# Ids prepared as pairs of 16 bit numbers, six banks for the first group's counts, two count blocks moved by one instruction

## The reference

```
mask   = (sequence_ids != 0)                                  # 2048 users x 200 ids
pooled = sum over the ids of item_embeddings[max(id - 1, 0)] * mask / max(number of ids that are not 0, 1)
user_rep  = pooled @ W_rec.T + b_rec
retrieved = item_embeddings[retrieved_indices].mean(axis=1)   # 50 per user
gate   = sigmoid(concat(user_rep, retrieved) @ gate_W.T + gate_b)
fused  = gate * user_rep + (1 - gate) * retrieved
logits = fused @ proj_W.T + proj_b                            # 2048 x 12500
```

## Time and profile before

| | us |
|---|---|
| median of 3 timed runs | 2159.99 (2159.94 to 2164.19) |
| the profiled execution | 2149.49 |
| its span (first to last instruction) | 2147.7 |
| TensorE busy | 2066.8 (96%) |
| VectorE busy | 1569.8 (73%) |
| ScalarE busy | 817.0 (38%) |
| GpSimd busy | 1126.0 (52%) |

### The profile page before, as it was taken

How to read it: one execution, slowest core, us unless ns; L and a number is a source line. 1 busy time by engine, 2 the same in 40 slices (tenths; PEclk the granted TensorE clock), 3 DMA queues, 4 the chain that set the end, 5 groups by cost and what they waited for, 6 DMA issues and landing times.

```text
span 2147.7 us, 32019 instructions
## 1 busy us (share of the span) xinstructions
PE 2066.8 (96%) x12722; PEld 1062.3 (49%) x12722; DVE 1569.8 (73%) x1677; ACT 817.0 (38%) x1009; POOL 1126.0 (52%) x830
## 2 busy tenths in 40 slices
PE   5669999999999999999999999999999999999999
PEld 4555555555555555444444444444444444444444
DVE  8999999888888887444577777687778864544544
ACT  5866676445544545435211212232212122221121
POOL 5676551788678855657366767666676500000000
PEclk8569999999999999999999999999999999999999
DMA  8999997999899988879589998887899974576665
GB/s 304 333 235 299 280 321 251 301 264 252 242 266 250 250 303 281 309 243 338 170 299 324 312 315 300 301 279 260 316 327 350 367 246 149 196 232 235 222 224 182
DMA packets 222050, 586.82 MB, mean 273 GB/s; under 512 B 21840, under 2 KB 121040, under 8 KB 218576
## 3 DMA queue, kind: packets, MB, share of 16 engines
q1 hardware_dynamic: 91424, 264.21, 36.2%
q0 software_dynamic: 77632, 218.16, 35.8%
q10 hardware_dynamic: 52848, 102.41, 12.6%
HBM read 448.21 MB, written 136.48 MB: 272 GB/s over the span
## 4 chain that ended last, share of the span: by engine, by line
PE 80%; DVE 8%; POOL 6%; ACT 3%; issue 2%; DVEq 2%; DMA 1%; ACTq 0%
PE banks_ps L1345 45%; PE banks_ps L1238 23%; PE banks_ps L1220 6%; PE banks_ps L1250 6%; POOL gathered L586 4%; DVE row_hots L685 2%; POOL gathered L564 2%; ACT counts L1003 2%; DVE keys L687 2%; DVE ring L692 1%; ACT counts L997 1%; DVEq L729 0%; DMA gathered<-emb,ret_rows 0%; PE banks_ps L1268 0%; DVE gathered L730 0%
## 5 line engine op out<-in xcount | busy, mean ns | idle before, releaser
L1238 PE MATMUL banks_ps<-mid,ring 128*128 128x512 f16 x3136 | 725.0, 379 | 1.7 <-ACT mid L1021 1.7
L564 POOL DMA_INDIRECT gathered<-emb,ret_rows x460 | 569.5, 1238 | 292.8 <-DVE gathered L730 137.2
L1345 PE MATMUL banks_ps<-counts,keys 128*128 128x500 f16 x2400 | 510.5, 374 | 0.0
L1345 PE MATMUL banks_ps<-counts,mid 128*128 128x500 f16 x2400 | 508.4, 374 | 1.5 <-DVE counts L776 1.5
L1238 PEld LDWEIGHTS banks_ps<-mid,ring 128*128 128x128 f16 x3136 | 292.0, 98 | 306.9 <-issue 3.2
L586 POOL DMA_INDIRECT gathered<-emb,ret_rows x184 | 348.1, 1892 | 130.0 <-ACT ring L1011 55.3
L963 DVE SCALAR_TENSOR_TENSOR ring<-banks_ps,out_scale,counts 128x1000 f32<-128x1000 f32 x160 | 201.1, 1257 | 259.7 <-PE banks_ps L1345 258.4
L1345 PEld LDWEIGHTS banks_ps<-counts,mid 128*128 128x128 f16 x2400 | 233.0, 97 | 274.0 <-DVE counts L776 2.0
L685 DVE TENSOR_TENSOR row_hots<-pair_columns,keys 128x2048 f16<-128x2048 f16 x256 | 313.0, 1223 | 71.2 <-PE banks_ps L1220 70.1
L1345 PEld LDWEIGHTS banks_ps<-counts,keys 128*128 128x128 f16 x2400 | 231.6, 97 | 269.6 <-DVE counts L776 0.2
L1220 PE MATMUL banks_ps<-keys,row_hots 128*128 128x98 f16 x4096 | 282.4, 225 | 59.4 <-DVE keys L687 44.5
(11 more groups left out here) (130 smaller groups left out, 878.0 us busy)
## 6 DMA issues: line engine op xcount, KB each, us to landing
logits<-ring ACTq DMA_DIRECT2D x99, 1000.0 KB, 6.5
ring<-emb_parts SPq DMA_DIRECT2D x147, 512.0 KB, 6.3
counts<-proj_t SPq DMA_DIRECT2D x75, 1000.0 KB, 5.7
counts<-emb SPq DMA_DIRECT2D x14, 1792.0 KB, 10.5
emb_parts<-ring SPq DMA_DIRECT2D x49, 512.0 KB, 6.4
mid<-emb SPq DMA_DIRECT2D x46, 512.0 KB, 7.4
counts<-proj_b SPq DMA_DIRECT2D x75, 250.0 KB, 4.6
gathered<-emb,ret_rows POOLq DMA_INDIRECT x660, 6.3
```

The source lines that it names most:

```text
L564: pool.indirect_dma_start(slots[group][:, a], None, source, column(block, r * SLOT + a))\
L1238: last = pe.matmul(pooled_ps[:, m], ring_v[:, p % RING, c, part, m * P:(m + 1) * P], cvt[:, p % CVT, c], start=(i == 0 and c == 0 and part ...
L1345: last = pe.matmul(banks_ps[:, logit_bank(n), 0:W], fused[g // 2][:, f, k, at_user:at_user + P], strip_parts[:, t % 2, w, k, :], start=(k ...
```

## The change

**Ids.** `prepare_ids` had eight instructions on 1024 elements of 32 bit inputs: subtract 1, find ids of 0 (as 512, added to the row so that it meets no column), find present ids, clamp, low bits, high bits, add, convert. It now has one with two tensors (negative ids wrap once, as `max((x < 0), x)` writes it), one that clamps, subtracts 1 and writes 16 bit numbers, two bitwise ones that work on pairs of these as 32 bit words (512 elements), and three on 16 bit numbers in and out (rows, chunks, present). An absent id is -1 now, whose chunk of 127 meets none of the 98 columns. The wait for `present_counted` stands ahead of the last of them, behind the two conversions.

**Banks.** The quads of group 0 use six banks, 1 to 6, in turn, and a quad waits for the move of the quad six before it. Later groups use banks 4 to 6 as before; their first three quads wait for all quads of group 0.

**Move.** In group 0 ScalarE moves a unit's two quads, from two neighbouring banks, by one instruction of 784 elements (`move_first`). The pieces of the table are squared after the same units as before: where one stood between a unit's two quads it now stands behind the unit.

```diff
+FIRST_BANKS = 6
+BOTH = (P - 1) * 65537
+        item_i = part_of(keys, 0, 2048, I16)
+        row_i = part_of(keys, 2048, 2048, I16)
+        asked_i = part_of(keys, 4096, 4096, I32)
+        column_i = part_of(keys, 4096, 2048, I16)
...
+        def first_bank(q):
+            return 1 + q % FIRST_BANKS
+        def count_bank(q):
+            return first_bank(q) if q < pl.quads else KH + q % COUNT_BANKS
...
             def prepare_ids(g):
                 dve.drain()
                 dve.wait_ge(ids_in, 16 * (g + 1))
-                dve.tensor_scalar(chunk_of, raw, -1.0, None, ALU.add)
-                dve.tensor_scalar(chunk_key, raw, 0.0, ABSENT, ALU.is_equal, ALU.mult)
+                dve.scalar_tensor_tensor(asked_i, raw, 0.0, raw, ALU.is_lt, ALU.max)
+                dve.drain()
+                dve.tensor_scalar(item_i, asked_i, float(pl.items), -1.0, ALU.min, ALU.add)
+                dve.drain()
+                dve.tensor_scalar(row_i.bitcast(I32), item_i.bitcast(I32), BOTH, None, ALU.bitwise_and)
+                dve.tensor_scalar(column_i.bitcast(I32), item_i.bitcast(I32), 7, BOTH, ALU.logical_shift_right,
+                                  ALU.bitwise_and)
+                dve.drain()
+                dve.tensor_copy(row_key, row_i)
+                dve.tensor_copy(chunk_key, column_i)
                 if g > 0:
                     dve.wait_ge(present_counted, g)
-                dve.tensor_scalar(present[:], raw, 0.0, None, ALU.not_equal)
-                dve.drain()
-                dve.tensor_scalar(clamped, chunk_of, 0.0, float(pl.items - 1), ALU.max, ALU.min)
-                dve.drain()
-                dve.tensor_scalar(raw, clamped, P - 1, None, ALU.bitwise_and)
-                dve.tensor_scalar(clamped, clamped, 7, None, ALU.logical_shift_right)
-                dve.drain()
-                dve.tensor_tensor(row_key, raw, chunk_key, ALU.add)
-                dve.drain()
-                dve.tensor_copy(chunk_key, clamped)
+                dve.tensor_scalar(present[:], item_i, -1.0, None, ALU.not_equal)
                 dve.drain().then_inc(ids_ready, 1)
...
+            def move_first(u):
+                act.wait_ge(quad_counted, 2 * (u + 1))
+                at = first_bank(2 * u)
+                act.activation(counts_v[:, 0, :, u * UNIT:(u + 1) * UNIT].rearrange("p c (b u) -> p c b u", b=2),
+                               banks_ps[:, at:at + 2, 0:QUAD * NQ].rearrange("p b (u c) -> p c b u", u=QUAD),
+                               ACT.Copy).then_inc(quad_moved, 2)
...
-            for q in range(pl.quads):
-                move_quad(q)
-                if q % 7 == 6 and squared < NORM:
+            for u in range(pl.units):
+                move_first(u)
+                if squared < min(NORM, 2 * (u + 1) // 7):
                     square_norm(squared)
                     squared += 1
-                if q in (119, 121, 123):
-                    if q == 119:
+                if u in (59, 60, 61):
+                    if u == 59:
                         act.wait_ge(scale_made, 1)
-                    split_high((q - 119) // 2)
+                    split_high(u - 59)
...
             def count_quad(q):
                 pe.wait_ge(hots_made, q // 2 + 1)
-                if q >= COUNT_BANKS:
-                    pe.wait_ge(quad_moved, q - COUNT_BANKS + 1)
+                if q >= pl.quads:
+                    pe.wait_ge(quad_moved, max(pl.quads, q - COUNT_BANKS + 1))
+                elif q >= FIRST_BANKS:
+                    pe.wait_ge(quad_moved, q - FIRST_BANKS + 1)
...
-                    to = count_ps[:, q % COUNT_BANKS, u * NQ:(u + 1) * NQ]
+                    to = banks_ps[:, count_bank(q), u * NQ:(u + 1) * NQ]
```

More of the change, by code:

```diff
@@ L11 @@
 I32 = mybir.dt.int32
+I16 = mybir.dt.int16
 U8 = mybir.dt.uint8
@@ L36 @@
 COUNT_BANKS = 3
-ABSENT = 512.0
+FIRST_BANKS = 6
+BOTH = (P - 1) * 65537
 F16_TOP = 14
@@ L221, in pooling_program @@
         raw = part_of(keys, 0, 4096, I32)
-        chunk_of = part_of(keys, 4096, 4096, F32)
-        clamped = part_of(keys, 4096, 4096, I32)
+        item_i = part_of(keys, 0, 2048, I16)
+        row_i = part_of(keys, 2048, 2048, I16)
+        asked_i = part_of(keys, 4096, 4096, I32)
+        column_i = part_of(keys, 4096, 2048, I16)
         row_key = part_of(keys, 8192, 2048, F16)
```

## The result

The changed kernel takes 2167.11 us (median of 22, one disturbed execution of 3621.36 among them; the others took 2163.86 to 2174.48, and the ratio is of these), the kernel before beside it 2161.19. The ratio is 1.0022, 95% interval 1.0012 to 1.0033. Forecast were 2150.4 us and 2144 to 2157: wrong in size and in sign.

What follows compares the result with a forecast made beforehand. VectorE was taken to bound the kernel up to some 220 us, TensorE behind that. The terms 6.65 + 1.26 - 0.33 + 0.72 + 1.26 = 9.56 us gave 2150.4 us, range 2144 to 2157.

Steps and rivals of the forecast that it cites:

- VectorE sets the pace up to 220 us: From the start to some 220 us VectorE is the limit, TensorE behind that; VectorE's losses ahead of pass 0 move the end.
- the stalls: First stage: six banks remove all waits around the table's squares, 0.95 us in each of 7 periods, 6.65 us gained.
- First ids: First preparation of ids, ahead of the first one-hots: 6.22 us becomes 4.96, 1.26 saved; bounds 2.8 saved to 0.4 lost.
- rival D: Preparation of ids: 16 bit instructions run at twice the rate, 0.44 us each, total 2149.6 us; chance 24%.
- The last move: ScalarE's last move ahead of pass 0 takes 0.83 us instead of 0.50: 0.33 us lost, bounds 0 and 0.5.
- rival A: First stage: the two-bank move is dear and ScalarE becomes the bound; 2165 us at twice the time per element; chance 6%.
- Group 1's stalls: Pass 0's start: shorter preparation of group 1 removes TensorE's stalls of 0.41 and 0.31 us, 0.72 us gained.
- Rival C: Start of pass 0: TensorE's half clock lasts into it by 16 products, 3.5 us lost, total 2153.9 us; chance 12%.
- Group 3's gathers: Pass 2: group 3's add comes earlier, so GpSimd's gathers land earlier: 1.26 us gained, bounds 0 and 1.32.
- rival E: Pass 2: the gathers behind group 3's preparation take no part, their term is 0, total 2151.7 us; chance 12%.
- What is late next is VectorE itself: First stage: once its stalls go, VectorE's own work sets the pace; ScalarE and TensorE keep up; no size of its own.
- Rival B: First stage: loads of the table's pieces set the pace, so the 6.65 us stay away, total 2157.0 us; chance 10%.

Runs made afterwards that it cites:

- e1_ids: The kernel before with the new preparation of ids alone (three banks, single moves): ratio 0.9976 to the kernel before, median 2156.74 us.
- e10_drain40: The changed kernel with one single drain of VectorE, ahead of unit 40: 2148.77 us, ratio 0.9950 to the kernel before.
- e9_sbuf: The kernel before with group 0's one-hots reading their columns as 32 bit numbers from SBUF: 2298.83 us, read for its trace alone.
- e6_drain8: The changed kernel with a drain of VectorE ahead of every eighth unit of group 0 (seven drains): ratio 0.9967 to the kernel before.
- e5_banks: The kernel before with six banks for group 0, old preparation of ids and single moves: 0.40% slower than the kernel before.
- e7_gate10: The changed kernel with each turn of GpSimd's gathers released by the tenth unit instead of the ninth: a gather held for 73.89 us; no total time given.
- e0_noids: The changed kernel with the old preparation of ids (six banks, two-bank moves): 0.55% slower than the kernel before.

## Why the prediction was wrong

- **VectorE sets the pace up to 220 us, and the stalls are worth 6.65 us: right.** Start of the stage 8.99 to 146.15 is 137.16 us, before 142.91, 5.75 less. The dearer move took 0.38 of the gain and the last counts at half clock 0.56 (1.49 for 0.93), so the stalls gave 6.7.
- **First ids: 1.26 us forecast, 2.0 measured.** 16 bit instructions took 0.42 us, not 0.69: rival D was right, and so is the table of the Trainium skill that stood beside it. The mis-sized term is the "nearest row". Alone, the ids gave 5 us (2.4 to 8.2), against 3.2 forecast for their three places.
- **The last move: 0.33 forecast, 0.38 measured** (2.11 - 1.73). Two banks in one instruction are not dear: rival A is out, at 0.82 us.
- **Group 1's stalls, 0.72 us: gone as forecast.** From 150 to 180 us TensorE is busy for 30.00 us.
- **Rival C (half clock into pass 0) was seen, but isn't the change's loss.** The first 48 products took 13.07 us at a granted clock of 0.81 (146 to 160 us); at 1.73 for eight they would take 10.4. In the traces of the nine other timed kernels they took 11.91 to 13.39 us, 12.78 of them in e1_ids, whose pass 0 is 225.03 us long all the same. Only the trace of the kernel before had full clock there (10.52).
- **Group 3's gathers, 1.26 us: nothing came (rival E).** In e10_drain40, whose gathers aren't late, GpSimd's wait behind the earlier add is shorter (1.63 us for the 3.66 of the earlier trace rows), yet VectorE waits the same 3.47 us as in the earlier trace rows and TensorE loses 1.81 us there instead of 1.32.
- **The step that failed is "What is late next is VectorE itself", and with it that what is won ahead of pass 0 moves the end.** For the start of pass 0 the step held (146.15 for 146.3). But GpSimd was late, and the sum had no term for its gathers in this stage: they were put at nothing without a reason. With VectorE's stalls gone one gather was held for 54.77 us, the gathers missed then were made beside pass 0's table loads, and pass 0 took 17.15 us more. Rival B had the loads of the first stage in view, with a price of 6.65 us at most, and no rival had GpSimd. The prediction's own last sentence did describe what came: a first pooling product ahead of 147 with an end that doesn't follow, and "something behind it gives the time back".

Could it have been read beforehand? A part of it. These are two timelines of the kernel before, GpSimd's and VectorE's at one place:

```profile
25.39 1.72 POOL L583 DMA_INDIRECT gathered<-emb,ret_rows  x1 [0.30 <-issue]
27.41 0.95 POOL L583 DMA_INDIRECT gathered<-emb,ret_rows  x1 [0.31 <-issue]
```

```profile
27.73 1.23 DVE L685 TENSOR_TENSOR row_hots<-pair_columns,keys 128x2048 f16<-128x2048 f16 x1 [0.57 <-PE banks_ps L1220]
```

The same kind of gather takes 1.72 us beside unbroken one-hots and 0.95 where VectorE stalls, at 27.2 to 27.7. So the two engines' dependence could be read. That stalls sped GpSimd up in general could not: next to the stalls that ended at 42.83 and 57.92 a gather took 2.37 us. And that a stretch can turn into a stop of 54 us is in no row there. With the stop out of the way the time comes near the forecast: e10_drain40 took 2148.77 us, 10.9 below the kernel before beside it (7.3 to 14.5 by the interval), where 9.56 less and 2150.4 were forecast. In part that is luck: the ids gave 0.7 us more than their term and the gathers of group 3 nothing for 1.26, and the traces show only 6.4 us of it at the end of pass 0 (372.92 for 379.31).

Left open: why that one gather is held and others aren't. All held ones started behind 3.56 to 3.86 us of waiting (11.17 in e9_sbuf), none straight behind another gather. But waits as long didn't always lead to a hold: in e6_drain8 a gather behind 3.56 us passed in 1.61 us (at 73.19, with no gap beside it), in the kernel before one behind 3.71 (at 80.25), in e10_drain40 one behind 3.37, and in the changed kernel the very first, behind 12.96 us, took 2.06. A timing within VectorE's unit may decide; no run shows it. So what is shown is that a gap ends a hold, and that none of the six kernels with stalls or repeated gaps had a gather above 3.10 us; after its one drain e10_drain40 had no gather behind more than 1.46 us of waiting, so one drain sufficed there perhaps by chance.

## What to carry to other kernels

When a change fills the last gaps of VectorE, ask which engine used them. A gather of GpSimd can be held for as long as VectorE's instructions with two inputs in SBUF follow each other without a gap. Try a planned gap of 0.2 us now and then in a long row of these (one or seven drains were enough here), or one input in PSUM. And look at transfers for the stage behind: 50 us without gathers in a stage that didn't mind cost 17 us in the next one.

## What the runs showed of the hardware

- An indirect gather of GpSimd beside a row of VectorE's two-input instructions mostly took 1.72 us, or was held: for 54.74 to 73.89 us in four kernels, for 14.63 where a drain ended it, and for 192.50 beside longer instructions; beside instructions with one input in PSUM it took 1.54 to 1.60 us (0.94 to 1.16 without the addition) and was never held in the one trace of that kind.
- Held gathers ended 1.4 to 1.5 us behind a gap in VectorE's row, be it of 0.17 us (a drain, e10_drain40) or of some 0.01 to 0.02 us (a wait for late counts; the changed kernel, e5_banks, e7_gate10), or 1.5 to 1.6 us behind the start of the scale's small instructions (e0_noids, e9_sbuf).
- VectorE's 16 bit instructions with 1024 elements from one tensor took 0.42 us, with 16 bit integers in and 16 bit floats out, against 0.69 with 32 bits in.
- One ScalarE instruction over two PSUM banks (784 elements in four dimensions) took 0.82 us against 0.50 for 392: 0.33 more for the second bank.
